# A selective-scan layer on one Trainium2 core: drive of the odd steps as a product with a diagonal, and the block loop written out

## What is computed

```python
xc = jax.nn.silu(conv4(tn @ W_in_x + b))          # tn: layer norm over channels
dbl = xc @ W_x                                     # 8 ranks, 16 B, 16 C per token
delta = jax.nn.softplus(dr @ dt_w + dt_b)
def step(h, inputs):
    d_t, B_t, C_t, x_t = inputs
    dA = jnp.exp(d_t[:, :, None] * A)
    h = dA * h + (d_t * x_t)[:, :, None] * B_t[:, None, :]
    y = jnp.einsum('nds,ns->nd', h, C_t)
    return (h, y)
y = (ys + xc * D) * jax.nn.silu(z);  out = y @ W_out + b_out + x
```

## Time and profile before

| | us |
|---|---|
| median of three runs | 9,539.61 |
| lowest and highest | 9,535.70 and 9,547.48 |
| the profiled execution, its own time | 9,544.83 |
| its span, first to last instruction | 9,543.0 |
| granted TensorE clock, mean over the span | 0.986 |

### The profile page before, as it was taken

How to read it: one execution, slowest core, us unless ns; L and a number is a source line. 1 busy time by engine, 2 the same in 40 slices (tenths; PEclk the granted TensorE clock), 3 DMA queues, 4 the chain that set the end, 5 groups by cost and what they waited for, 6 DMA issues and landing times. The chain is left out here.

```text
span 9543.0 us, 181899 instructions
## 1 busy us (share of the span) xinstructions
PE 8679.4 (91%) x54525; PEld 6752.8 (71%) x54525; DVE 8330.0 (87%) x8144; ACT 7711.4 (81%) x13926; POOL 8059.3 (84%) x3865
## 2 busy tenths in 40 slices
PE   7998999999899999989999999999799999999899
PEld 4666666666666666666666666666688888888788
DVE  5998999999889999998999999899788888888766
ACT  6998999999899999999999999999555555555577
POOL 5999999999999999999999999999688888888500
PEclk9999999999999999999999999999899999999999
DMA  3333333333333333333333333333200100010255
GB/s 90 113 115 113 109 117 109 113 110 119 109 108 114 115 114 108 117 112 110 110 119 113 110 116 109 114 108 120 76 32 31 36 31 32 31 36 31 78 185 178
DMA packets 648652, 933.96 MB, mean 98 GB/s; under 512 B 79961, under 2 KB 277601, under 8 KB 643553
## 3 DMA queue, kind: packets, MB, share of 16 engines
q1 hardware_dynamic: 647904, 924.64, 31.0%
HBM read 778.38 MB, written 146.04 MB: 97 GB/s over the span
## 5 line engine op out<-in xcount | busy, mean ns | idle before, releaser
L1045 POOL TENSOR_TENSOR prod<-state,c_all 128x1024 f32<-128x1024 f32 x1280 | 3028.2, 2370 | 176.8 <-DVE state L919 167.9
L919 DVE TENSOR_TENSOR_SCAN state<-decay_d,drive_d 128x1024 f32<-128x1024 f32 x1024 | 2337.2, 2282 | 158.0 <-issue 86.0
L1034 POOL TENSOR_TENSOR drive_d<-du,b_all 128x1024 f32<-128x1024 f32 x1024 | 2422.9, 2366 | 53.0 <-DMA b_all<-bc_rows 48.9
L919 DVE TENSOR_TENSOR_SCAN state<-decay_r,drive_r 128x1024 f32<-128x1024 f32 x1024 | 2325.0, 2271 | 28.4 <-PE drive_r L591 26.1
L604 PEld LDWEIGHTS y_acc<-ident,prod 128*128 128x128 f32 x16384 | 1861.5, 141 | 627.8 <-issue 532.5
L604 PE MATMUL y_acc<-ident,prod 128*128 128x128 f32 x16384 | 2152.3, 275 | 40.6 <-POOL prod L1045 36.8
L1342 DVE SCALAR_TENSOR_TENSOR sum_d<-bank_d,filt,sum_d 128x512 f32<-128x512 f32 x2470 | 1679.6, 744 | 268.2 <-PE bank_d L1250 241.3
L1389 POOL TENSOR_TENSOR sum_p<-sum_p,scaled 128x1024 f32<-128x1024 f32 x650 | 1551.7, 2387 | 261.5 <-ACT scaled L1300 229.5
L747 ACT ACTIVATE ub<-ut,bt 128x256 f32<-128x256 f32 x4096 | 1739.0, 499 | 16.1 <-PE drive_r L591 16.1
L1300 ACT ACTIVATE scaled<-bank_p,filt 128x512 f32<-128x512 f32 x1560 | 944.1, 688 | 734.5 <-PE bank_p L1250 660.0
L734 ACT ACTIVATE decay_d<-delta,neg_a 128x504 f32<-128x504 f32 x2048 | 1312.0, 674 | 64.0 <-DVE state L919 63.2
(11 more groups left out here) (155 smaller groups left out, 14712.8 us busy)
## 6 DMA issues: line engine op xcount, KB each, us to landing
c_all<-bc_rows SPq DMA_DIRECT2D x1280, 256.0 KB, 3.3
b_all<-bc_rows SPq DMA_DIRECT2D x1024, 256.0 KB, 3.8
ys<-row_spectra SPq DMA_DIRECT2D x130, 256.0 KB, 2.8
column_sums<-tt SPq DMA_DIRECT2D x130, 256.0 KB, 2.2
x_in<-in_x_dram SPq DMA_DIRECT2D x64, 512.0 KB, 4.5
x_res<-in_x_dram SPq DMA_DIRECT2D x64, 512.0 KB, 4.6
x_rows<-x SPq DMA_DIRECT2D x64, 512.0 KB, 4.5
row_spectra<-z SPq DMA_DIRECT2D x64, 512.0 KB, 3.7
```

The source lines that it names most:

```text
L919: dve.tensor_tensor_scan(state[n % NT][:].rearrange("p h t -> p (h t)"), decay[:].rearrange("p h w t -> p (h w t)"), drive[:].rearrange("p ...
L1034: pool.tensor_tensor(drive_d[place_of(DSTEPS, n, ND)][:], du[:, :, q * HT:(q + 1) * HT], b_all[slot][:].unsqueeze(1).to_broadcast([P, 2, HT]),
L1045: pool.tensor_tensor(prod[n % NP][:], state[n % NT][:], c_all[slot][:].unsqueeze(1).to_broadcast([P, 2, HT]), ALU.mult).then_inc(s["prod_g ...
```

## The change

1. The drive of an odd step is no longer a scaled copy of `ut` turned around. ScalarE scales the identity instead (`spread_b`: four activations of 128 elements), which gives for each group of 128 tokens a diagonal matrix of B, `b_diag`. PE multiplies `ut` (as stationary operand) with that diagonal (`mix_drive`: eight fp32 products of 128 by 128, no transposes), which gives channels by tokens scaled by B, in the same `drive_r`.
2. The waits that protect `ut` move with its reader: PE waits for its copies instead of ScalarE, and VectorE's copy waits until the products of the old `ut` are done.
3. The loop over pairs of slots is gone: all 68 slots are written out, with constant numbers in all waits.

```diff
--- before.py
+++ after.py
@@ -159,18 +159,8 @@
 
 def slots(eng, body, blocks):
     rounds = (0, 0)
-    for m in range(-2, 2):
-        slot = Slot(m, True, m >= -1, m >= 0, m >= 1, False, rounds)
-        body(slot, m % 2)
-        rounds = tuple(r + k for r, k in zip(rounds, slot.size))
-    per = tuple(sum(j[3] == bank for j in JOBS) for bank in range(2))
-    with eng.Fori(0, (blocks - 4) // 2) as j:
-        for i in range(2):
-            body(Slot(j * 2 + 2 + i, True, True, True, True, True,
-                      tuple(j * (2 * k) + (r + k * i) for r, k in zip(rounds, per))), i)
-    rounds = tuple(r + k * (blocks - 4) for r, k in zip(rounds, per))
-    for m in range(blocks - 2, blocks + 2):
-        slot = Slot(m, False, m < blocks - 1, m < blocks, m <= blocks, True, rounds)
+    for m in range(-2, blocks + 2):
+        slot = Slot(m, m < blocks - 2, -1 <= m < blocks - 1, 0 <= m < blocks, 1 <= m <= blocks, m >= 2, rounds)
         body(slot, m % 2)
         rounds = tuple(r + k for r, k in zip(rounds, slot.size))
 
@@ -438,7 +428,7 @@
         ut = [sb(f"ut{q}", [P, 4, DI]) for q in range(2)]
         b_all = [sb(f"b_all{i}", [P, HT]) for i in range(NB)]
         c_all = [sb(f"c_all{i}", [P, HT]) for i in range(NCR)]
-        ub = [sb(f"ub{i}", [P, 4, DI]) for i in range(NS_UB)]
+        b_diag = [sb(f"b_diag{i}", [P, 4, P]) for i in range(NS_UB)]
@@ -582,15 +572,14 @@
                 pe.matmul(c_bank[:], wt["pick"][:, n % NS, :], c_rows[q][:], start=True,
                           stop=True).then_inc(s["c_full"], 1)
 
-            def turn_drive(step):
+            def mix_drive(step):
                 M, p, n = step
                 scanned(pe, *before_in(RSTEPS, M, n, 1))
-                need(pe, s["ub_done"], upto(RSTEPS, M, n))
+                need(pe, s["b_diag_done"], upto(RSTEPS, M, n))
                 for hf in range(2):
                     for g in range(4):
-                        mm = pe.matmul(drive_r[:, hf, g * P:(g + 1) * P],
-                                       ub[place_of(RSTEPS, n, NS_UB)][:, g, hf * P:(hf + 1) * P], wt["ident"][:],
-                                       start=True, stop=True, is_transpose=True)
+                        mm = pe.matmul(drive_r[:, hf, g * P:(g + 1) * P], ut[n // NS][:, g, hf * P:(hf + 1) * P],
+                                       b_diag[place_of(RSTEPS, n, NS_UB)][:, g, :], start=True, stop=True)
                 mm.then_inc(s["drive_r_done"], 1)
 
             def add_state(step):
@@ -705,8 +694,10 @@
 
             def body(S, p):
                 for n in range(NSTEP):
+                    if n == next(k for k in RSTEPS if k >= NS) - 1 and S.scan:
+                        taken(pe, S, "ut01", "ut11")
                     if n + 1 in RSTEPS and S.scan:
-                        turn_drive(S.step(n + 1, p))
+                        mix_drive(S.step(n + 1, p))
                     if n - 1 in BY_VECTOR and S.scan:
                         broadcast_c(S, S.step(n - 1, p))
                     jobs(S, p, 2 * n)
@@ -715,6 +706,8 @@
                     if n in SKIP_AT and S.scan:
                         add_skip(p, (n - ADD_BEHIND) // NS, SKIP_AT[n])
                     jobs(S, p, 2 * n + 1)
+                if S.front:
+                    taken(pe, S, "ut00", "ut10")
 
             slots(pe, body, blocks)
 
@@ -737,16 +730,16 @@
                         ACT.Exp, scale=wt["neg_a"][:, hf, st:st + 1])
                 last.then_inc(done, 1)
 
-            def scale_u(step):
+            def spread_b(step):
 
                 M, p, n = step
                 q, st = n // NS, n % NS
                 M0, n0 = before_in(RSTEPS, M, n, NS_UB)
                 need(act, s["drive_r_done"], upto(RSTEPS, M0, n0))
                 for g in range(4):
-                    last = act.activation(ub[place_of(RSTEPS, n, NS_UB)][:, g, :], ut[q][:, g, :], ACT.Copy,
+                    last = act.activation(b_diag[place_of(RSTEPS, n, NS_UB)][:, g, :], wt["ident"][:], ACT.Copy,
                                           scale=bt[q][:, g, st:st + 1])
-                last.then_inc(s["ub_done"], 1)
+                last.then_inc(s["b_diag_done"], 1)
 
             def take_rows(S, M, q):
                 misc = full(act, S, f"xp{q}")
@@ -894,10 +887,10 @@
                         make_decay(S.step(n + 2, p))
                     if (n + 3) % NSTEP in RSTEPS and S.step(n + 3, p):
                         if (n + 3) % NSTEP == RSTEPS[0]:
-                            taken(act, S, "bt0", "ut00", "ut10")
+                            taken(act, S, "bt0")
                         if n + 3 == next(k for k in RSTEPS if k >= NS):
-                            taken(act, S, "bt1", "ut01", "ut11")
-                        scale_u(S.step(n + 3, p))
+                            taken(act, S, "bt1")
+                        spread_b(S.step(n + 3, p))
                     others(S, p, 2 * n + 1)
 
             act.preload_act_table_set(TABLES)
@@ -947,6 +940,8 @@
 
             def take_ut(S, hf, q):
                 misc = full(dve, S, f"ut{hf}{q}")
+                M = S.m if q else S.m + 1
+                need(dve, s["drive_r_done"], upto(RSTEPS, M - 1, NS * (q + 1) - 1))
                 dve.tensor_copy(ut[q][:, :, hf * P:(hf + 1) * P],
                                 misc[:].rearrange("p (g d) -> p g d", g=4)).then_inc(take(S, f"ut{hf}{q}"), 1)
```

More of the change, by code:

```diff
@@ L464, in layer0 @@
             rows_done rows_stored rows_landed c_high_done softplus_done delta_done du_done c_full decay_d_done decay_r_done
-            ub_done drive_d_done drive_r_done scan_done prod_v_done prod_g_done added y_copied stats_done mv_done
+            b_diag_done drive_d_done drive_r_done scan_done prod_v_done prod_g_done added y_copied stats_done mv_done
             less_mean_done rstd1_done shift1_done z1_done yo_done zeroed""".split()
```

## The result

The changed kernel takes **9,952.09 us** (median of four runs, 9,950.72 to 9,953.92) against 9,537.66 us for the kernel before on the same chip: a ratio of 1.0434, 95% interval 1.0416 to 1.0452, that is 414 us more (0.0416 x 9,538 = 397 to 0.0452 x 9,538 = 431). The forecast was 9,990 us with a range of 9,850 to 10,160, "slower" with 0.96.

The account below looks back on a forecast made before the run. TensorE was taken to bound each block's middle part, with waits elsewhere. Products +595 us, jumps -145, ScalarE and ut waits 0: +450 on the profiled 9,544.83 gives 9,995, less 5.2 for the median: 9,990 us, range 9,850 to 10,160.

Parts of the forecast that it names:

- PE's price: Products instead of transposes in all odd steps: 9.3 us more a block, +595 us over 64 blocks.
- ScalarE's relief: Activations of 128 instead of 256 elements free 6.7 us of ScalarE's work a block; counted as worth nothing in time.
- the jumps' gain: Writing the loop out removes 29 jumps of 4.99 us each: -145 us.
- TensorE sets the pace of the middle part: Between scans 5 and 18 of a block, PE is busy 43.84 of 43.95 us, without a hole, while VectorE waits.
- +6.4 us for seven products in the middle: Seven odd steps between scans 5 and 18, at +0.91 us each, fall wholly on the path.
- The sign named for it: Middle part near 50 us; growth clearly below 6.4 us would mean that other engines set its pace.
- +2.9 us for the other nine: Outside the middle part, nine odd steps bring 8.2 us a block, of which PE's waits there hide 5.3.
- The waits for ut: Waits moved to PE and VectorE at steps 1 and 17 and ut's copies; over long before asked for, cost 0.
- the second (straight code gives the gain back): Across all blocks written out, the 145 us return as small stalls: 10,135 us; chance 0.05.
- the third (faster): PE only looks full throughout the block and ScalarE counts: 9,395 us or less, down to 9,043; chance 0.03.
- the fourth (a product four times its transposes): In every odd step a product step takes 3.5 us, 42 us more a block: about 11,760 us; chance 0.01.
- the first (waits on top): Outside the middle only scan waits are filled: 12.1 us a block, 10,169 us, or 10,329 with none; chance 0.10 beyond range.

Follow-up runs that it names:

- e10: The changed kernel timed once more without an edit, on the same chip as e9: 9,955.94 us, ratio 1.0441 to the kernel before.
- e3: The changed kernel with eight transposes of ut in place of the products (B left out, identity still scaled): 9,332.45 us, ratio 0.9805 to the kernel before.
- e1: The kernel before with the loop written out and nothing else changed: 9,408.09 us, ratio 0.9885 to the kernel before.
- e4: The changed kernel with ut and b_diag in the one-pass type fp32r: 9,366.43 us, ratio 0.9841 to the kernel before.
- e6: Straight code with the product in odd steps 1, 3, 5 and 21 to 31, scaled copies and transposes in 7 to 19: 9,579.33 us, ratio 1.0048.
- e7: Straight code with the product in odd steps 1, 21, 25 and 31 alone, scaled copies and transposes in the others: 9,497.00 us, ratio 0.9959.
- e5: Straight code with the product only in odd steps 7 to 19, scaled copies and transposes in the nine others: 9,818.76 us, ratio 1.0301.
- e9: e3 with each transpose of ut made twice into the same place, 16 matmul records a step, no true product: 9,917.83 us, ratio 1.0400.
- e8: The kernel before with four slots in each loop round instead of two, 14 jumps instead of 29: 9,455.60 us, ratio 0.9925.
- e2: The changed kernel with the loop of the kernel before put back: 10,051.79 us, ratio 1.0560 to the kernel before.

## Why the prediction was right, and where its terms were off

The forecast, 9,990 us, was 38 us too high. Its direction and its largest term, +0.91 us a product step where PE has no hole, are confirmed by the runs. That it came so close is in part luck, for three terms were off and cancel in part: PE's price was forecast as 595 us and is 623 (e10 less e3), ScalarE's relief as 0 and is 76, the jumps' gain as 145 and is 92 to 129. Together they would move the sum by -32 to +5 us; the result lies 38 below it.

- **TensorE sets the pace of the middle part: shown.** e1, e3, e4, e6 and e7, with ScalarE and PE's other parts changed, all have 43.66 to 43.69 us there; the change, e5 and e9, with 16 records a step there, have 48.90 to 49.14.
- **A product is two records of 0.112 us, +0.91 us a step: shown** by the profile after (16 in 1.95 us), by e9 (records alone) and e4 (one record). 
- **+6.4 us for seven products in the middle: shown** by e5's 6.4 us a block. The sign named for it was off: by the scans' cut that part grew by 5.2 us (43.95 to 49.13) or 5.5 against e1, not by 6.4, and growth clearly below 6.4 was to show that other engines set it. They don't: PE has no hole there, and eight of the 56 new records fall behind scan 18 (327 records against 279 in the middle).
- **+2.9 us for the other nine: near in size, wrong in part in its composition.** e6 has 2.7, but with ScalarE's relief in these steps. With the relief on both sides, all sixteen cost 623 / 64 = 9.7 us, which leaves 3.3 for the nine if seven cost 6.4. Gone, as said: POOL's prod (0.5), delta (0.4), VectorE's prod (0.3) and most of the scan waits (1.8 to 0.4). Not filled: the wait for the first sq, 1.1 us still, which I had counted as filled by the product between mean and variance; e7 shows the same for single scan waits. Gone though I had left it standing: cent (1.0) altogether, and half of the second sq. Of these, delta and the half of the second sq are gone in e3 too, without any product, so they go with ScalarE's relief.
- **ScalarE: the price was right (0.295 us forecast, 0.293 measured), the value 0 was wrong.** e3 shows 75.6 us, 1.2 us a block, all outside the middle. The step that failed is the sentence that the rest is "already PE's own work and round trips": the round trips through ScalarE became shorter along with its work (delta 0.7 us to none, the second sq 0.5 to 0.3, y_tok 1.4 to 1.2).
- **The jumps: -145 us forecast, 92 to 129 us by e1's runs** (139 by the profiles). A jump was priced from two neighbouring blocks of one execution; the median branch is 6,174 ns, and the one read lasts 6,404. Besides, twelve of e1's blocks last 103.3 to 103.4 us instead of 102.2 with the clock's falls (below), some 14 us that the sum did not have.
- With the medians of e10 and e1, the products and ScalarE together come to 9,955.9 - 9,408.1 = 548 us, and less the 129 us of the jumps to 419; measured are 414.
- **The waits for ut** that moved to PE and VectorE cost nothing to be seen: none stands among PE's waits of block 27, and e1 and e3 differ in them as well and share the middle part.
- Of the rivals, the second (straight code gives the gain back) falls with e1, the third (faster) with e3, the fourth (a product four times its transposes) with the 1.95 us of the profile; the first (waits on top) wanted 12.1 us a block for the products where 623 / 64 = 9.7 are measured.

The other signs that I named hold but for the last: no long branch, 111 us blocks (110.82), the middle without a hole, 0.390 us for ScalarE's new line, and of "issue" holes PE has one of 0.4 us in a block. VectorE's idle time grew by 7.8 us in a block instead of 5 to 6.

## What to carry to other kernels

Where several engines show over 80%, cut the repeated unit of work where one of them has no hole, and price an edit part by part: the same product cost 0.91 us in one part of the block and 0.30 in another, and relief for an engine that isn't full in a part is worth nothing in it. Count matmul records, not calls: here an fp32 product of 128 by 128 is two, a transpose or an fp32r product one. And look at what the jump of a loop costs on TensorE; here writing out 60 slots was worth 92 to 129 us, and an edit that mixes such a gain with a loss should be taken apart.

## What was not expected of the hardware

**The branch of a loop is long on TensorE alone**, 4.4 to 6.2 us in the median in three kernels, and its length differs between kernels whose loops have the same structure. What it waits for is in the trace. For block 27 of the kernel before, the DMA rows of the stretch of the branch (3,029.5 to 3,035.9 us) are:

```profile
q1 hardware_dynamic: 1509, 1.64, 95.0%
q8 instruction: 1, 0.02, 1.0%
q14 instruction: 2, 0.02, 0.7%
```

In all 72 long branches of the three loop kernels exactly one packet of the instruction queue q8, 16 KB, starts and ends inside the branch, and the branch ends 1.3 to 1.6 us after the packet does; over the whole program such packets come 18 to 19 us apart in the median. The length of the branch follows the time until the packet starts: 3.8 us in the median in the kernel before, 2.9 in e8, 1.9 in e2, for branches of 6.2, 5.2 and 4.4 us. q8 carries TensorE's instructions: the changed kernel has 8,192 more matmul records than e1, as many more weight loads, and 64 more packets in q8 (385 against 321), while q14's stay the same (259 and 256). So at a jump PE waits for a block of its instructions, and e2's branches are shorter because the packet starts sooner. No run changed this; it is read from the 72 branches. Straight code has such packets as well (291 between 300 and 6,500 us of e1) and no such hole. Why the packet starts late stays open. The kernel's own transfers fill the DMA engines meanwhile (the 95.0% above), which would delay it, but no run varied them.

**The clock falls in straight code, without a hole of several microseconds.** In ten blocks of the changed kernel TensorE's granted clock drops to the lower level for a few microseconds, and the block is 1.7 us longer. In block 61 it looks like this; the last row is add_state's, eight transposes in 1.91 us:

```profile
6968.35 1.10 PE L622 MATMUL job_bank<-sq,mean_w 128*128 128x512 f32 x2 [1.09 <-ACT sq L795]
...
6969.38 0.50 PE L572 MATMUL job_bank<-c_rows,pick 48*128 48x512 f32 x1
...
6970.14 1.07 PE L659 MATMUL job_bank<-ident,du 128*128 128x128 f32 x4 [0.26 <-ACT sq L800]
...
6971.01 1.91 PE L593 MATMUL y_acc<-ident,prod 128*128 128x128 f32 x8
```

The stretch from 6,970 to 6,974 us has a mean granted clock of 0.57 (third column from the end):

```profile
6970.00:6974.00 4.00, 3.86 (x17) 3.66 (x18) 3.93 (x3) 3.24 (x7) 4.00 (x3) 0.57 0.03 11
```

The same place in block 27, with the same waits, keeps its clock and takes 1.04 us:

```profile
3194.32 1.04 PE L593 MATMUL y_acc<-ident,prod 128*128 128x128 f32 x8
```

Before the fall stand two waits, 1.09 and 0.26 us, with short work between. In the kernel before, 26 of the 29 jumps, with holes of some 4 us, have a fall, and 6 more stand elsewhere. In e4 it falls more often than in e3: over the window from 300 to 6,500 us its mean is 0.99 where e1, e3 and the changed kernel round to 1.00, and half of its blocks last 101.4 to 103.0 us instead of 101.0. The two profiled executions are 9,355.3 - 9,330.7 = 25 us apart, as their blocks add up to; the medians differ by 34. e3 first, then e4:

```profile
300.00:6500.00 6200.00, 5796.87 (x35758) 4257.94 (x35756) 5838.92 (x4528) 5541.03 (x10962) 5926.91 (x2940) 1.00 0.37 116
```

```profile
300.00:6500.00 6200.00, 5837.21 (x35628) 4334.54 (x35627) 5815.76 (x4513) 5522.17 (x10913) 5909.65 (x2930) 0.99 0.37 116
```

What decides between the places where it falls and those where it holds stays open. The Trainium skill (TensorE: Matmul & The Clock Gate, Why this matters for your kernels) advises against long idle gaps between bursts of matmuls, lest the throughput drop. The trace agrees behind a jump (a 4 us hole, and at 26 of 29 the clock fell); in block 61 of after the clock fell with no single gap over 1.09 us.
